# Folding the keys of a group in three blocks instead of four, in a cross attention of 1024 queries on 64 keys

## What is computed

```python
qh = (q @ Wq + bq).reshape(16, 1024, 16, 64)
kh = (k @ Wk + bk).reshape(16, 64, 16, 64)
vh = (v @ Wv + bv).reshape(16, 64, 16, 64)
attn = einsum('bqhd,bkhd->hbqk', qh, kh) * mask
attn = exp(attn - max(attn)) * mask
attn = attn / (sum(attn, -1) + 1e-15)
out = einsum('hbqk,bkhd->bqhd', attn, vh).reshape(16, 1024, 1024) @ Wo + bo
x = out + q
return (x - mean(x)) / sqrt(var(x) + 1e-05) * gamma + beta
```

## Time and profile before

| | |
|---|---|
| median of three runs | 1606.03 us (1605.92 to 1606.26) |
| the profiled execution | 1606.72 us, of which 1604.8 us span from first to last instruction |
| granted TensorE clock, mean | 0.999 |
| PE busy | 1586.6 us, 99% of the span |
| DVE, ACT busy | 1167.4 us (73%), 886.1 us (55%) |
| scores phase | from the start to about 872 us |

### The profile page before, as it was taken

One profiled execution on the slowest core, in us unless ns is written; L12 is line 12 of the kernel. 1 busy time (PEld: TensorE's weight loads), 2 busy tenths in 40 slices (PEclk: granted clock), 3 DMA queues, 4 the chain that ended last, 5 costly groups with the idle time before them and its releaser, 6 DMA issues. The chain is left out here.

```text
span 1604.8 us, 31907 instructions
## 1 busy us (share of the span) xinstructions
PE 1586.6 (99%) x11117; PEld 769.3 (48%) x11118; DVE 1167.4 (73%) x2397; ACT 886.1 (55%) x1356; POOL 584.2 (36%) x884
## 2 busy tenths in 40 slices
PE   7999999999999999999999999999999999999998
PEld 4555455455554555555544444444444444444443
DVE  7767475765665756656655998888888888888885
ACT  6555454554554545545445666666666666666652
POOL 0000000000000000000000498888888888888875
PEclk9999999999999999999999999999999999999999
DMA  6584565562844656638444966556655566655522
GB/s 230 191 278 145 164 212 178 175 213 98 270 144 153 211 178 180 209 103 279 144 152 129 370 262 262 218 221 243 255 206 222 218 250 261 246 216 222 205 79 79
DMA packets 100469, 323.80 MB, mean 202 GB/s; under 512 B 10128, under 2 KB 14352, under 8 KB 90640
## 3 DMA queue, kind: packets, MB, share of 16 engines
q1 hardware_dynamic: 100368, 322.32, 57.7%
HBM read 192.26 MB, written 130.02 MB: 201 GB/s over the span
## 5 line engine op out<-in xcount | busy, mean ns | idle before, releaser
L115 PE MATMUL ps_o<-u,p_hi 128*128 128x512 f16 x1024 | 388.8, 380 | 1.2 <-DMA u<-u_halves 1.2
L106 PE MATMUL ps_s<-x_hi,g_hi 128*128 128x512 f16 x1024 | 388.7, 380 | 0.9 <-issue 0.3
L116 PE MATMUL ps_o<-u,p_hi 128*128 128x512 f16 x1024 | 388.1, 379 | 0.0
L117 PE MATMUL ps_o<-u,p_lo 128*128 128x512 f16 x1024 | 388.1, 379 | 0.0
L108 PE MATMUL ps_s<-x_hi,g_lo 128*128 128x512 f16 x1024 | 388.1, 379 | 0.0
L107 PE MATMUL ps_s<-x_lo,g_hi 128*128 128x512 f16 x1024 | 388.1, 379 | 0.0
L631 ACT ACTIVATE s<-ps_s,c_bias 128x512 f32<-128x512 f32 x256 | 176.5, 689 | 355.4 <-PE ps_s L108 353.2
L866 POOL PARTITION_ALL_REDUCE key_max<-early_max x1 | 0.7, 712 | 853.5 <-DVE early_max L788 853.5
L1174 ACT ACTIVATE p_hi<-ps_bc 128x512 f16<-128x512 f32 x256 | 152.1, 596 | 161.7 <-DVE ps_bc L1322 161.6
L779 DVE TENSOR_TENSOR score_max<-score_max,tile_max 128x1 f32<-128x1 f32 x257 | 40.7, 158 | 271.1 <-ACT s L631 268.9
L1456 POOL TENSOR_TENSOR y<-y,gamma_b 128x512 f32<-128x512 f32 x124 | 158.2, 1275 | 86.1 <-ACT y L1187 86.1
(11 more groups left out here) (140 smaller groups left out, 2450.4 us busy)
## 6 DMA issues: line engine op xcount, KB each, us to landing
scores<-s SPq DMA_DIRECT2D x30, 2048.0 KB, 7.5
x<-xT_in SPq DMA_DIRECT2D x32, 1024.0 KB, 10.3
u_halves<-u_out SPq DMA_DIRECT2D x256, 128.0 KB, 3.0
u<-u_halves SPq DMA_DIRECT2D x16, 2048.0 KB, 11.6
s_more<-scores SPq DMA_DIRECT2D x16, 2048.0 KB, 9.7
y<-x_in SPq DMA_DIRECT2D x32, 1024.0 KB, 7.7
out<-y SPq DMA_DIRECT2D x31, 1024.0 KB, 5.1
s<-scores SPq DMA_DIRECT2D x14, 2048.0 KB, 9.4
```

Source lines behind the costliest of these rows:

```text
L106: pe.matmul(out, lhs_hi, rhs_hi, start=first, stop=False)
L115: pe.matmul(out, lhs_hi, rhs_hi, start=False, stop=False, skip_group_check=True)
L116: pe.matmul(out, lhs_hi, rhs_lo, start=False, stop=False, skip_group_check=True)
L117: return pe.matmul(out, lhs_lo, rhs_hi, start=False, stop=False, skip_group_check=True)
```

## The change

Outside group 0's own folds the eight pairs of a group go in three blocks: (0, 1, 2) behind tile 3 of unit 3, (3, 4) behind tile 6 of unit 3 with `bias` behind it, and (5, 6, 7) before tile 1 of unit 0. The third pair of a block takes the two banks `ps_k` in addition to the four of `ps_f` (`key_bank`). A block waits once, for all banks, instead of once for each pair; the last block also waits for `c_ready`, since `bias` has used `ps_k`. ACT and DVE read the same banks in the same blocks; DVE's part of `bias` moves from tile 5 to tile 6 with it, and ACT has a second wait, at pair 3. The number of matmuls, activations and transfers does not change.

```diff
--- before.py
+++ after.py
@@ -269,11 +269,22 @@
 
 
 
+        BLOCKS = ((0, 1, 2), (3, 4), (5, 6, 7))
+
+        def key_bank(first, p, h):
+
+            if first:
+                return ps_f[(2 * p + h) % GBANKS]
+            of = next(block for block in BLOCKS if p in block)
+            return (ps_f + ps_k)[2 * of.index(p) + h]
+
+
+
         def late_folds(first):
-            return {1: (2, 3), 2: (4, 5), 4: (6, 7)} if first else {1: (4, 5), 3: (6, 7)}
-
-
-        early_folds = {3: (0, 1), 5: (2, 3)}
+            return {1: (2, 3), 2: (4, 5), 4: (6, 7)} if first else {1: BLOCKS[2]}
+
+
+        early_folds = {3: (0, 1, 2), 6: (3, 4)}
         FIRST_EARLY = 2
 
         def u_tile(g, q, j):
@@ -456,8 +467,14 @@
                 if first and p % 2 == 0:
                     pe.wait_ge(w_lo_done, 5 + p // 2)
 
-                pe.wait_ge(f_lo_done, g * FT + 2 * p + 2)
-                tiles = [ps_f[(2 * p + h) % GBANKS] for h in range(2)]
+
+                if first:
+                    pe.wait_ge(f_lo_done, g * FT + 2 * p + 2)
+                elif p in (0, 3, 5):
+                    pe.wait_ge(f_lo_done, g * FT + 2 * p + GBANKS)
+                    if p == 5:
+                        pe.wait_ge(c_ready, 2 * g + 1)
+                tiles = [key_bank(first, p, h) for h in range(2)]
                 for c in range(DC):
                     cols = slice(c * P, (c + 1) * P)
                     for k, (weights, keys) in enumerate(((wq_hi, kv_hi), (wq_lo, kv_hi), (wq_hi, kv_lo))):
@@ -584,14 +601,14 @@
                 act.wait_ge(kv32_done, NP * (i + 1))
                 act.activation(kv_hi[:, :, :], kv32[:, :, :], ACT.Copy, scale=scale).then_inc(kv_hi_done, 1)
 
-            def round_g(g, p):
-                if p == 0 and not (isinstance(g, int) and g == 0):
-
-                    act.wait_ge(s_summed, (g * UNITS + 1) * NP + EARLY)
+            def round_g(g, p, first):
+                if p in (0, 3) and not first:
+
+                    act.wait_ge(s_summed, (g * UNITS + 1) * NP + (EARLY if p == 0 else EARLY + 2))
                 for h in range(2):
                     i = 2 * p + h
                     act.wait_ge(f_summed, g * FT + i + 1)
-                    act.activation(of_folded(g_hi, p, h), by_key_halves(ps_f[i % GBANKS]),
+                    act.activation(of_folded(g_hi, p, h), by_key_halves(key_bank(first, p, h)),
                                    ACT.Copy, scale=G_SCALE / (W_SCALE * K_SCALE)).then_inc(f_hi_done, 1)
 
             def round_u(g, q, first):
@@ -626,7 +643,7 @@
                     if u == 0:
 
                         for pair in late_folds(first).get(1 if first and p == 0 else 0 if first and p == 1 else p, ()):
-                            round_g(g, pair)
+                            round_g(g, pair, first)
                     act.wait_ge(s_summed, n * NP + p + 1 + 2 * NP)
                     act.activation(s32[:, u % 2, p, :], ps_s[p % SBANKS][:, :], ACT.Identity, bias=c_bias[:, p, u // UB:u // UB + 1],
                                    scale=1 / (G_SCALE * X_SCALE)).then_inc(s_out, 1)
@@ -640,7 +657,7 @@
                         split_ctx(g + 1)
                     if u == UNITS - 1 and not last and p in early_folds:
                         for pair in early_folds[p]:
-                            round_g(g + 1, pair)
+                            round_g(g + 1, pair, False)
                     if p == NP // 2 and not (last and u == UNITS - 1):
                         round_x(g, u + 1)
                     if first and u < 3 and p in split_behind[u]:
@@ -678,8 +695,8 @@
             first_keys_out(3)
             round_kv(0, K_SCALE)
             round_x(0, 0)
-            round_g(0, 0)
-            round_g(0, 1)
+            round_g(0, 0, True)
+            round_g(0, 1, True)
             split_weight(5)
             split_weight(6)
             split_weight(7)
@@ -720,11 +737,11 @@
                 dve.scalar_tensor_tensor(kv_lo[:, :, :], kv32[:, :, :], scale, kv_hi[:, :, :],
                                          ALU.mult, ALU.subtract).then_inc(kv_lo_done, 1)
 
-            def split_g(g, p):
+            def split_g(g, p, first):
                 for h in range(2):
                     i = 2 * p + h
                     dve.wait_ge(f_hi_done, g * FT + i + 1)
-                    dve.scalar_tensor_tensor(of_folded(g_lo, p, h), by_key_halves(ps_f[i % GBANKS]),
+                    dve.scalar_tensor_tensor(of_folded(g_lo, p, h), by_key_halves(key_bank(first, p, h)),
                                              G_SCALE / (W_SCALE * K_SCALE), of_folded(g_hi, p, h),
                                              ALU.mult, ALU.subtract).then_inc(f_lo_done, 1)
 
@@ -793,12 +810,12 @@
                     if u == 0 and first:
 
                         for pair in late_folds(first).get(p + 1, ()):
-                            split_g(g, pair)
+                            split_g(g, pair, first)
                         if p == 0:
                             mask(0, 0)
                     if u == 0 and not first and p in late_folds(first):
                         for pair in late_folds(first)[p]:
-                            split_g(g, pair)
+                            split_g(g, pair, first)
                     dve.wait_ge(s_out, n * NP + p + 1 + SBANKS)
                     raise_max(n * NP + p, p)
                     if last and u == UNITS - 1 and p == 0:
@@ -817,7 +834,7 @@
                         split_ctx(g + 1)
                     if u == UNITS - 1 and not last and p in early_folds:
                         for pair in early_folds[p]:
-                            split_g(g + 1, pair)
+                            split_g(g + 1, pair, False)
                         if p == max(early_folds):
                             bias(g + 1)
                     if p == NP // 2 and not (last and u == UNITS - 1):
@@ -844,8 +861,8 @@
                 split_weight(i)
             split_kv(0, K_SCALE)
             split_x(0, 0)
-            split_g(0, 0)
-            split_g(0, 1)
+            split_g(0, 0, True)
+            split_g(0, 1, True)
             split_weight(5)
             bias(0)
```

## The result

| | before | after |
|---|---|---|
| median of eleven runs each | 1606.26 us (1605.58 to 1607.2) | 1610.38 us (1610.01 to 1610.8) |
| profiled execution, and its span | 1606.72 us, 1604.8 us | 1610.75 us, 1608.9 us |
| ratio after to before | | 1.0025, 95% interval 1.0018 to 1.0033 |

The change is slower by 4.1 us. The forecast was 1610.1 us, in a range from 1607.5 to 1613.

What follows compares the result with a forecast made beforehand. PE was taken to bound the kernel, working 99% of the span. From 1606.03 us, 1.4 us saved at block edges and 5.5 us lost at five loop turns gave 1610.1 us, range 1607.5 to 1613.

Steps and rivals of the forecast that it cites:

- The term that decides: Turn of PE's loop over groups: queued work hiding the branch falls from 3.8 to 2.7 us; 5 x 1.1 = 5.5 us lost.
- the length of the branch: PE's branch back in the loop over groups: taken to stay at 3.56 to 3.75 us.
- The edges: PE's switches to half rows and back around blocks: 0.20 us saved in each of groups 1 to 7, 1.4 us together.
- The estimate from the constant: Half-row switches on PE, from a 166 ns matmul constant: 0.33 us for two drains, 2.3 us for seven blocks.
- ACT and DVE: Three pairs taken out at once beside PE's products: no cost; tightest at the third block, with 1.16 us slack.
- Rival A: Turn of PE's loop costs what it did, its length following queued work; 1604.6 us, not slower; 16%.
- B: Turn: branch grows by 0.3 to 1 us, or third block overtakes pages on their way; 1611.6 to 1615 us; 8%.
- C: Third block: DVE reaches c_ready later than its slack, at 2 us lateness 1.7 us on top, 1611.8 us; 3%.
- D: PE's half-row switches dearer by more than double, and no longer turn of the loop; 1602.5 us; 1%.
- The late product: First product on PE after the branch at the loop's turn: 1.2 to 1.5 us late, five times.
- the idle time of PE with "issue" named: Sign at the five turns of PE's loop: the late product shows as idle time attributed to "issue".
- The sum: Whole kernel: 1606.03 - 1.4 + 5.5 = 1610.1 us; on the profiled execution 1610.8 us.

Runs made afterwards that it cites:

- the kernel without any cover: Kernel before the change, four blocks of two pairs, with the second early block and bias moved behind tile 7, right before the turn: 1636.55 us against 1606.4, ratio 1.0193.

## Why the prediction was right, point by point

- **The term that decides** was the branch with one tile of cover instead of two. The branch began 0.07 us before the first product of the last tile, as forecast, all five turns lengthened, and the passage into group 7 did not. The step from "how many instructions ahead" to a time is what carried it. In the old place 33 instructions are still to start when the branch begins, and a pair of them takes 0.216 us. In the new one it is 35 to 38 at the register work 0.1 us before the branch, but 11 to 14 of them are dense ones of bias that pass in this 0.1 us, and 24 are left.
- **Its size**: 5.1 us in the traces, 5.5 forecast. The mis-sized part is the length of the branch. It was taken to stay; it lasted 3.33 to 3.95 us, 3.57 in the mean, against 3.67 before. By program and turn it lies anywhere from 3.28 to 4.04 us, also with the same cover, and its mean over the turns of a program from 3.42 to 3.72. So the 0.2 us on each branch that the range allowed was about right for a mean, if not generous: with the block behind tile 6 and nothing else the mean is 0.25 us below the kernel before.
- **The edges**: 1.5 us measured, 1.4 forecast, 0.21 us for a block instead of 0.20, the same for a block of three. The estimate from the constant in the Trainium skill, "TensorE: Matmul & The Clock Gate", Single matmul latency, 2.3 us, was too high.
- **ACT and DVE** at no cost: c_bias ended 242.24 - 236.29 = 5.95 us after its block began, as forecast to the hundredth, and at the passage without a turn into group 1 (c_bias to 136.04, third block at 137.32) 1.28 us were left of a forecast 1.16.
- **Rival A** (the turn costs the same whatever the cover) fell by the change itself, and by the kernel without any cover. That the branch ended near the end of its cover before was chance: in the kernel after it ends 1.3 us behind it (238.04 + 3.95 against 240.71). **B** (the branch grows by 0.3 to 1 us) did not come: the longest, 3.95 us at the first turn, is 0.25 us longer than that turn's before, and the mean fell. **C** and **D** did not occur.
- **Wrong in details**: The late product was to come 1.2 to 1.5 us late at each turn; it came 1.02 to 1.63 us late, and in that band only twice. And I expected the idle time of PE with "issue" named. The profile named ACT. The releaser is the last semaphore event that the waiting instruction could have waited for; the wait for `s_out` stands on the first product of the tile, and ACT had met it 0.75 us earlier. This is a case in which the engine named had long been done and what held PE was the sequencer.
- The sum was made against 1606.03 us and the medians of eleven runs moved that to 1606.26, so that 4.1 us of forecast difference met 4.1 us measured. In the traces the parts are 5.1 - 1.5 = 3.6 us, and the remaining 0.4 us is the start of the program. Part of the close agreement is luck.

## What to carry to other kernels

A hardware loop has a price where it turns, and what hides it is what the engine still has queued when its sequencer comes to the branch. That is a number of instructions and not of microseconds, so keep long instructions in front of the turn and dense small ones (here bias and the folds) away from it, or write the loop out, or keep its body small enough to be held: here three blocks without the move gained 1.7 us, and with it they lost 4.1. And before you believe the engine that an idle time names, compare the end of its last instruction with the start of the waiting one.

## What the runs showed of the hardware that I had not expected

- The branch back of PE's loop took 0.22 to 0.24 us with 1594 instructions in the body and 3.3 to 4.0 us with 1818 or more. With 1786 it was short at one turn out of five, in one and the same execution.
- Every one of the 34 long branches held one fetch of 16 KB and lasted 2.1 to 2.9 us longer than the fetch itself; no short taken one held any.
- Behind gaps of 3.4 us and more at a turn the granted clock of PE was half for 3.4 or 6.8 us, and at the first turn this cost half as much again as the gap; behind the gaps of 1.0 to 1.6 us at the turns of the change it was not.
- The waits don't show the work of PE's sequencer: of the gaps made by the branch, the ten of 1.0 to 1.6 us in two kernels were put down to ACT, the short ones and those of 3.4 us and more to "issue".
